# Attention's result kept channel-major: packed and spread by transfers, divided and split by GpSimd

## The reference

```
xn  = layernorm(x)
qkv = xn @ W_attn + b_attn ; q, k turned by a rotary table
att = softmax(causal(q k^T / 4)) ; y = att @ v          # per head
s   = y @ W_proj + b_proj
h   = silu(xn @ Wg^T) * (xn @ Wu^T) ; g = silu(h @ Wd^T)  # 768 hidden
out = x + s * g
```

## Time and profile before

| | |
|---|---|
| time, median of 3 runs | 1243.81 us (1241.86 to 1245.1) |
| profiled execution, its own time | 1244.25 us |
| its span, first to last instruction | 1242.5 us |
| TensorE busy (matmuls) | 1173.0 us, 94% |
| VectorE | 1060.9 us, 85% |
| ScalarE | 911.7 us, 73% |
| GpSimd | 693.9 us, 56% |
| share of the chain that ended last | TensorE 57%, VectorE 20%, GpSimd 9%, ScalarE 7%, issue 5% |

### The profile page before, as it was taken

The page is one execution under the profiler, slowest core; times in us unless marked ns, Lnnn a source line. Parts: engine busy times, 40 slices in busy tenths (PEclk is TensorE's granted clock), DMA queues, the critical chain, the costliest instruction groups (busy, mean ns, idle before and its releaser), DMA issues.

```text
span 1242.5 us, 27851 instructions
## 1 busy us (share of the span) xinstructions
PE 1173.0 (94%) x9820; PEld 494.2 (40%) x9820; DVE 1060.9 (85%) x3250; ACT 911.7 (73%) x1736; POOL 693.9 (56%) x859
## 2 busy tenths in 40 slices
...
GB/s 171 69 149 2 1 104 53 103 25 74 51 140 28 32 111 36 129 19 27 103 58 106 21 76 53 137 31 32 111 36 129 19 27 103 54 77 27 44 2 51
DMA packets 56048, 81.45 MB, mean 66 GB/s; under 512 B 8766, under 2 KB 34756, under 8 KB 55908
## 3 DMA queue, kind: packets, MB, share of 16 engines
...
...
## 4 chain that ended last, share of the span: by engine, by line
PE 57%; DVE 20%; POOL 9%; ACT 7%; issue 5%; DMA 0%; SPq 0%; POOLq 0%; DVEq 0%; ACTq 0%
PE ring L844 27%; PE acc L835 12%; PE st L784 8%; DVE ring L1203 6%; PE ring L811 5%; DVE mx_a L1207 4%; ACT pexp L1042 2%; POOL hf L1530 2%; PE ring L917 2%; DVE ln L1237 2%; DVE ga L1270 1%; DVE parts L1261 1%; POOL hT L1539 1%; POOL xn L536 1%; ACT yT L1049 1%
## 5 line engine op out<-in xcount | busy, mean ns | idle before, releaser
L1042 ACT ACTIVATE pexp<-st 128x512 f32<-128x512 f32 x1152 | 624.9, 598 | 141.0 <-PE st L784 137.9
L1203 DVE CUSTOM_DVE_ANT_0 ring<-ring,tri 128x512 f32<-128x512 f32 (+3 forms) x1024 | 470.2, 522 | 30.5 <-PE ring L811 30.0
L1500 POOL TENSOR_SCALAR_AFFINE_SELECT pexp<-pexp 128x512 f32<-128x512 f32 x256 | 158.5, 638 | 405.0 <-ACT pexp L1042 405.0
L1207 DVE TENSOR_REDUCE mx_a<-ring 128x1 f32<-128x512 f32 x512 | 328.1, 683 | 17.8 <-PE ring L811 15.2
L835 PE MATMUL acc<-pexp,v_pad 128*17 128x512 f32 (+3 forms) x3072 | 303.7, 490 | 4.1 <-POOL pexp L1500 2.4
L811 PE MATMUL ring<-k_st,q_st 56*128 56x512 f16 (+4 forms) x1536 | 243.7, 326 | 14.7 <-POOL k_st L1622 3.7
L784 PE MATMUL st<-q_st,k_st 58*128 58x512 f16 (+3 forms) x1536 | 233.9, 331 | 6.7 <-ACT pexp L1042 3.7
L784 PEld LDWEIGHTS st<-q_st,k_st 58*128 58x128 f16 x1536 | 61.3, 93 | 267.7 <-ACT pexp L1042 183.8
L1530 POOL TENSOR_TENSOR hf<-ga,ups 128x512 f32<-128x512 f32 x96 | 122.5, 1276 | 37.4 <-issue 37.4
L835 PEld LDWEIGHTS acc<-pexp,v_pad 128*17 128x17 f32 x3072 | 61.3, 96 | 138.1 <-issue 121.1
L1539 POOL TENSOR_TENSOR hT<-hf,hT 128x512 f16<-128x512 f32 x96 | 111.3, 1160 | 3.4
...
## 6 DMA issues: line engine op xcount, KB each, us to landing
...
parts_scratch<-parts SPq DMA_DIRECT2D x32, 256.0 KB, 3.0
xo<-in_x SPq DMA_DIRECT2D x32, 256.0 KB, 2.9
out<-xo SPq DMA_DIRECT2D x32, 256.0 KB, 2.2
xn<-in_x SPq DMA_DIRECT2D x7, 1024.0 KB, 7.4
q_st<-mT SPq DMA_DIRECT2D x126, 4.0 KB, 1.7
```

The source lines that it names most:

```text
L1042: nc.scalar.activation(pexp[:, GH * (n % NSET) + j, :], st[:, (GH * n + j) % NST, :], ACT.Exp, scale=1.0 / (QK_SCALE * np.sqrt(D))).then_i ...
L1203: top_ = nc.vector.tensor_tensor_reduce(out=src, in0=src, in1=tri[:, CH - w:CH], scale=1.0, scalar=NEG, op0=ALU.add, op1=ALU.max, accum_ou ...
L1207: top_ = nc.vector.reduce_max(dst, src, AX.X)
L1500: nc.gpsimd.affine_select(out=t, in_=t, compare_op=ALU.is_ge, fill=0.0, base=0, pattern=[[0, GH], [1, P]], channel_multiplier=-1).then_inc ...
```

## The change

`YT` and `FT` go from the body of the kernel for all batches but the last, which keeps them for its own attention. In their place:

- `YS` (8 per batch, SyncE): for a group and `qc`, one transfer stores the four heads' sums in DRAM and four move 16 channels each into their packed rows of `yp` (128 channels of a pair of groups by tokens). `copy_acc` now waits for the moves out of the same half of `yT` one group before.
- per pair of groups `kt`: `YG` loads the 8 heads' sums as 128x64, `YR` (VectorE) takes their reciprocal, `YB` stores it, `YC` spreads it in 8 transfers, one per head, over 16 partitions each (`rb`, 128x1024). All but `YR` are SyncE's.
- `YN`, `YH`, `YL` (GpSimd, per pair and `qc`): `yp * rb`, its copy to 16 bits, the remainder, each 128x512, into a wider `ynT`. `FP` waits for these.
- `TASKS`, `END_TASKS` and `LAG` are written anew; `LNR`'s lag grows from 0 to 2, `LNA`'s falls from 1 to 0, `LNS`'s from 1 to 0, `LNS` 0 stands in slot 2 and not 4.

The code that is new, and the wait in `copy_acc`:

```diff
+            def move_y(i, g, qc):
+                unit = pair_unit(i, g)
+                pair = pair_number(i + (g == 2), g // 2, qc)
+                wait(sp, acc_out, 2 * unit + qc + 1)
+                if g % 2 == 0:
+                    wait(sp, y_low, pair - 2)
+                stand(sp, sp_stand)
+                sp.dma_start(sums_dram[GH * (g % 2):GH * (g % 2) + GH, qc * CH:qc * CH + CH], yT[D:P:32, qc, :]).then_inc(y_moved[qc], 16)
+                for j in range(GH):
+                    row = 64 * (g % 2) + D * j
+                    sp.dma_start(yp[row:row + D, qc, :], yT[32 * j:32 * j + D, qc, :]).then_inc(y_moved[qc], 16)
+            def gather_sums(i, kt):
+                for qc in range(2):
+                    sp.wait_ge(y_moved[qc], 16 * (GH + 1) * pair_units(i, kt))
+                stand(sp, sp_stand)
+                sp.dma_start(ysum[:, :], sums_dram.rearrange("h (a r) -> (h a) r", r=4 * D)).then_inc(sums_in, 16)
+            def store_inverse(i, kt):
+                sp.wait_ge(inv_ready, pairs_before(i, kt) + 1)
+                stand(sp, sp_stand)
+                sp.dma_start(inv_dram.rearrange("h (a r) -> (h a) r", r=4 * D), yinv[:, :]).then_inc(inv_out, 16)
+            def spread_inverse(i, kt):
+                sp.wait_ge(inv_out, 16 * (pairs_before(i, kt) + 1))
+                wait(sp, y_scaled, 2 * pairs_before(i, kt))
+                stand(sp, sp_stand)
+                for h in range(2 * GH):
+                    sp.dma_start(rb[D * h:D * h + D, :, :].rearrange("p q n -> p (q n)"),
+                                 inv_dram[h:h + 1, :].broadcast_to([D, T])).then_inc(rb_in, 16)
...
                 act.wait_ge(pv_done, STEPS * (4 * i + g) + (MIXED + 1 if qc == 0 else STEPS))
+                if i < B - 1 or g == 0:
+                    wait(act, y_moved[qc], 16 * (GH + 1) * (4 * i + g))
                 nc.scalar.activation(yT[:, qc, :], acc[:, :], ACT.Copy).then_inc(acc_out, 1)
...
+                if t[0] == "YR":
+                    dve.wait_ge(sums_in, 16 * (pairs_before(i, t[1]) + 1))
+                    stand(dve, dve_stand)
+                    return nc.vector.reciprocal(yinv[:, :], ysum[:, :]).then_inc(inv_ready, 1)
...
+                if t[0] in ("YN", "YH", "YL"):
+                    _, kt, qc = t
+                    pair = pair_number(i, kt, qc)
+                    if t[0] == "YN":
+                        pool.wait_ge(y_moved[qc], 16 * (GH + 1) * pair_units(i, kt))
+                        pool.wait_ge(rb_in, 16 * 2 * GH * (pairs_before(i, kt) + 1))
+                        stand(pool, pool_stand)
+                        nc.gpsimd.tensor_tensor(yp[:, qc, :], yp[:, qc, :], rb[:, qc, :], ALU.mult).then_inc(y_scaled, 1)
+                    if t[0] == "YH":
+                        if kt == 0 and i > 0:
+                            wait_ready(pool, kind, i, ("FP", 2 * qc + 1))
+                        pool.wait_ge(y_scaled, pair)
+                        nc.gpsimd.tensor_copy(ynT[:, qc, 0, kt, :], yp[:, qc, :]).then_inc(y_high, 1)
+                    if t[0] == "YL":
+                        pool.wait_ge(y_high, pair)
+                        nc.gpsimd.tensor_tensor(ynT[:, qc, 1, kt, :], yp[:, qc, :], ynT[:, qc, 0, kt, :], ALU.subtract)\
+                            .then_inc(y_low, 1)
```

More of the change, by code:

```diff
@@ L83 @@
 TASKS = {
[L84 to L94, removed]
@@ L175 @@
+    32: [("FT", 0, "end"), ("FT", 1, "end")],
     33: [("FP", 0, "end"), ("FP", 1, "end")],
 }
+PAIR = ("YG", "YR", "YB", "YC", "YN")
 def of_next(task):
-    return task[0] in ("LNS", "LNR", "LNA", "TX", "QK") or task in (("V", 0, 0), ("MT", 0))
+    return task[0] in ("LNS", "LNR", "LNA", "TX", "QK") or task[0] == "YS" and task[1] < 3 \
+        or task[0] in PAIR and task[1] == 0 or task in (("V", 0, 0), ("MT", 0))
 def of_last(task):
-    return task[-1] != "end" and (task[0] in ("FT", "FP") or task in (("DN", 1, 2), ("DN", 1, 3), ("YT", 3, 1)))
+    return task[-1] != "end" and (task[0] == "FP" or task in (("DN", 1, 2), ("DN", 1, 3)) or task[:2] == ("YS", 3)
+                                  or task[0] in PAIR and task[1] == 1)
@@ L189, in tasks_at @@
 def tasks_at(kind, slot):
-    tasks = END_TASKS if kind == "last" and slot >= END_FROM else TASKS
-    return [t for t in tasks.get(slot, [])
-            if not (kind == "first" and of_last(t)) and not (kind == "last" and of_next(t))]
+    found = [] if kind == "last" and slot >= END_FROM else TASKS.get(slot, [])
+    found = found + END_TASKS.get(slot, []) * (kind == "last")
+    return [t for t in found if not (kind == "first" and of_last(t)) and not (kind == "last" and of_next(t))]
 def has_max(kind, slot):
@@ L200 @@
     "scalar": {"TX": 0, "QD": 0, "QK": 0, "UPG": 0, "UPU": 0, "V": 0, "DN": 0, "FT": 0, "FP": 0, "MT": 0},
-    "vector": {"TX": 0, "QK": 0, "UPG": 0, "DN": 0, "FT": 0, "YT": 0, "LNS": 1, "BP": 0},
-    "gpsimd": {"LNR": 0, "LNA": 1, "XC": 1, "UPU": 2, "HI": 3, "LO": 4, "FP": 2, "FP_G": 3, "FP_X": 4},
-    "sync": {"QK": 2, "MT": 1, "FP": 5},
[3 rows of a table added]
 }
-PART_OF = {"HI": "UPU", "LO": "UPU", "FP_G": "FP", "FP_X": "FP"}
+PART_OF = {"HI": "UPU", "LO": "UPU", "FP_G": "FP", "FP_X": "FP", "YH": "YN", "YL": "YN"}
 def parts_at(engine, kind, slot, half):
@@ L240, in names_of @@
         return (0, 1)
-    return () if t[0] in ("LNS", "LNR", "LNA", "XC") else ("",)
+    return () if t[0] in ("LNS", "LNR", "LNA", "XC", "YS") + PAIR else ("",)
 ORDER = {"pro": PRO, "epi": EPI}
@@ L314, in th_buffer, with pair_unit, pairs_before, pair_units @@
     return BY["UPG+DN"].seen[kind].index(task) % 2
+def pair_unit(i, g):
+    return 4 * (i - (g == GROUPS - 1)) + g
+def pairs_before(i, kt):
+    return 2 * (i - kt) + kt
+def pair_units(i, kt):
+    return 4 * (i - kt) + 2 * kt + 2
+def pair_number(i, kt, qc):
+    return 4 * (i - kt) + 2 * kt + qc + 1
+def turned(kind, task):
+    return kind == "epi" or task[-1] == "end"
 def own_batch(i, task):
@@ L406, in build_program @@
         yn = sb("yn", [P, TT, C], fp32)
-        ynT = sb("ynT", [P, 2, 2, 2, 2 * P], fp16)
+        yp, rb = (yn[:, 4 * k:4 * k + 4, :].rearrange("p (q t) c -> p q (t c)", q=2) for k in range(2))
+        ynT = sb("ynT", [P, 2, 2, 2, CH], fp16)
+        ysum = sb("ysum", [P, 4 * D], fp32)
+        yinv = sb("yinv", [P, 4 * D], fp32)
         w_pr16 = sb("w_pr16", [P, 2, 2, C], fp16)
```

90 lines of the change are left out of this document (48 added, 42 removed), and 5 rows, old and new, of the table TASKS.

## The result

The changed kernel takes 1229.99 us (median of 4 runs, 1225.9 to 1233.76), the kernel before 1243.72 beside it: a ratio of 0.989, 95% interval 0.9848 to 0.9932. That is 1.1% faster, and inside the range of 1197 to 1235, but the gain is 13.7 us where the prediction's sum had 29.5. The profiled execution took 1226.92 us (span 1225.2). Of the 17.3 us between the two profiled spans, the six middle periods give 6.1 (22.8 forecast), the first body 2.0 and the last 6.5. The other 2.8 lie ahead of the first exponential, where traces of kernels with the same code there differ by more than that (76.5 to 81.1 us).

A forecast was written before the change was run, and what follows sets the result against it. TensorE's own work was the bound, VectorE close behind, GpSimd in one stretch. Middle batch -5.5 - 1.2 + 2.7 + 0.2 = -3.8, six -22.8, end bodies -5.5 and -1.2: -29.5, so 1214 us; 8-in-10 range 1197 to 1235.

The forecast's parts named there:

- TensorE, -5.5 a batch: TensorE in a full batch: 48 transposes fewer and nothing added, 5.5 us saved (5.2 to 6.1).
- GpSimd, +2.7: Slots 10 to 12 and 17: TensorE waits for GpSimd's masks and normalised input, 2.7 us a middle batch (0 to 5.5).
- SyncE at 0.2: SyncE's queue: loads held up behind the new stores and moves, 0.2 us a batch (0 to 1.5).
- the inverse's way: Reciprocal, store and spread for YN 1,0: there by s + 10, GpSimd arriving at s + 12.1, so no cost.
- `copy_acc` at nothing: Wait for a half of yT: free some 5 us after filling, wanted 36 us later, so no cost.
- The spread's landing: Transfers spreading the inverse for YN 1,0: landing estimated at 2.2 us, the 256 KB row.
- The formula that the prediction quotes for the input's load: Input's load: 2.0 us and bytes over 436 GB/s, 4.4 us; the prediction used the trace's 7.4.
- VectorE, -1.2 a batch: TensorE's waits for banks that VectorE empties: VectorE loses 7.6 us of work, giving back 1.2 (0 to 3).
- end bodies: First and last bodies: -5.5 us by fewer transposes and -1.2 by VectorE's relief, with no GpSimd cost.
- GpSimd takes nearly all: Rival, slots 10 to 12 and 17: stalls double to 5.5 us a batch, 1231 us; chance 0.14.
- The whole saving: Rival: GpSimd frees itself in time, so TensorE's saving comes whole, 1198 us; chance 0.22.

The follow-up runs named there:

- e4: Changed kernel with GpSimd's three passes of the new sets for pair 1 cut from 512 to 32 columns: 1219.95 us, 0.9805 of the kernel before.
- e5: Changed kernel with GpSimd's three passes of the new sets for pair 0 cut from 512 to 32 columns: 1231.8 us, 0.9892 of the kernel before.
- e8: Changed kernel with the reciprocal YR of pair 1 moved from slot 4 to slot 5: 1238.41 us, 0.9957 of the kernel before.
- e1: Changed kernel with only DN(0,2) moved behind the three QKs of slot 20: 1221.4 us, 0.9811 of the kernel before.
- b2: Kernel before the change with only DN(0,2) put ahead of the QKs of slot 20: 1255.7 us, ratio 1.0105.
- e9: Changed kernel with DN(0,2) behind slot 20's QKs and UPU(1,0) moved to slot 21, leaving UPU(1,1) in 22: 1204.36 us, 0.9685 of the kernel before.
- b1: Kernel before the change with only UPU(1,1) moved to slot 22 and UPU(1,2) to slot 24: 1269.03 us, ratio 1.0189.
- e3: Changed kernel with DN(0,2) behind slot 20's QKs, UPU(1,1) moved to slot 24 and UPU(1,2) to 25: 1214.14 us, 0.976 of the kernel before.

## Why the prediction was right in direction and half the size

**TensorE, -5.5 a batch: right.** By the matmuls' count and the spacing of their starts its own work fell by 5.2, the lower end of its range.

**GpSimd, +2.7: right in place and cause, 0.9 too much.** Slots 10 and 11 rose by 1.20 and 0.36 (1.6), and in slot 17 TensorE waits 0.2 for the normalised input: 1.8. TensorE's wait was 1.19 for 1.9, as the mask was 0.4 earlier and TensorE 0.4 later than reckoned; slot 11's 1.09 for 0.9. e4 gives the sets of pair 1 2.4 us a batch by themselves, e5 those of pair 0 nothing.

**SyncE at 0.2, the inverse's way and `copy_acc` at nothing: right.** In the first and the middle bodies no matmul of the changed kernel waits for a transfer, and `copy_acc` waits for none. The spread's landing was 2.3, on the estimate; all of it had arrived at s + 9.1 in the batch above and between s + 8.0 and s + 9.1 in the others, for s + 10. e8 puts the price of one slot more at 8 us. Issues of the changed kernel, columns as in the earlier trace rows:

```profile
xn<-in_x SPq DMA_DIRECT2D x7, 1024.0 KB, 8.1
...
yn<-inv_scratch SPq DMA_DIRECT2D x112, 64.0 KB, 2.3
```

The formula that the prediction quotes for the input's load, 4.4 us, is given in that section for transfers that GpSimd issues. These are SyncE's, and took 7.4 and 8.1.

**VectorE, -1.2 a batch: this is the step that failed.** The prediction took 7.6 us off VectorE and said "elsewhere the pressure falls". It counted what VectorE loses and never asked when what is left to it now runs, or in which order. With -5.2 for TensorE and +1.8 for GpSimd, the period of 143.74 leaves +2.1 a batch where -1.2 was forecast: a cost in place of a relief. Two things of the table were in the diff and got no term:

- `DN(0,2)` ahead of the `QK`s in slot 20: 1.57 us of waiting, 1.74 in the slot (e1), and 12.0 us in the kernel before with that edit alone (b2).
- `UPU(1,1)` and `UPU(1,2)` earlier, so that GpSimd's two-tensor passes meet VectorE's split of `MT` 3: a wait of 1.64 us, 2.17 in the slot (5.83 against e9's 3.66, some 1.6 net of what e9's move costs in slots 21 to 24), and the clock behind it. In the kernel before, that edit alone costs 25 us (b1). The held passes are also the greater part of why VectorE's busy time fell by 2.7 instead of 7.6: the twelve passes of a batch's four splits take 5.8 us for 2.3 before. The two reciprocals took 0.54 each, for an estimated 0.3; the other 0.9 isn't accounted for.

A table with the old order in those two places is e3, and it takes 1214.1, the forecast to the microsecond. That is luck: its middle period is 142.2 for a predicted 141.2, and its end bodies give 12.3 for 6.7. With the tasks placed better than in either table, e9 has 1204.4 and a middle period of 140.42. There the terms hold: -5.2 by TensorE, +1.8 by GpSimd, and the rest, 145.08 - 3.4 - 140.42 = 1.3 back, is the size of the forecast relief. It is a remainder, though, and e9 moved a task too. The end bodies were undersized: forecast at -6.7 together, they gave 2.0 (first) and 6.5 (last) in the changed kernel and 4.7 and 6.5 in e9. Why the last gives so much more than its 20 transposes wasn't tested; its own table of tasks was written anew as well.

**The rivals.** "GpSimd takes nearly all", 1231, comes nearest in time and was wrong in cause: of the waits that the change added, GpSimd's masks are the smaller part (14.5 us), and the larger is VectorE's (22.4). "The whole saving" fails on slots 10 and 11, where the sets of pair 1 cost 2.4 us a batch.

**The clock, which the prediction left out.** The changed kernel's runs lie 8 us apart. In the profiled one a single batch is 1.4 us longer than its neighbours; its window from slot 25 on has

```profile
748.00:756.00 8.00, 6.17 (x36) 2.31 (x37) 6.10 (x18) 3.62 (x8) 4.71 (x6) 0.79 0.13 27
```

a mean granted clock of 0.79, so it stood at the lower of its levels, 1.2 GHz instead of 2.4, for a part of them, right after TensorE had waited 1.63 us for VectorE. Slot 25 is 7.33 in that batch and 5.83 in the others. In e9, where the longest waits of the middle batches are gone, it falls in none of them.
